# A decoder's quantised attention: projections in tiles of 128 rows, an eighth of the sequences carried by the others

## The reference

```python
def _ln(x, w, b):                       # mean and variance over the last axis
    return (x - mu) * jax.lax.rsqrt(var + EPS) * w + b
def _fp8_linear_pertensor(x, wq, w_scale, in_scale):
    xq = _div_clamp_fp8(x, in_scale)
    return jnp.einsum('bsi,oi->bso', xq * in_scale, wq) * w_scale
...
ln_out = _ln(hidden_states, ln_w, ln_b)
q = _ln(_fp8_linear_pertensor(ln_out, wq, ...).reshape(b, s, g, hpg, d), qln_w, qln_b)
k = _ln(_fp8_linear_pertensor(ln_out, wk, ...).reshape(b, s, g, d), kln_w, kln_b)
v = _fp8_linear_pertensor(ln_out, wv, ...).reshape(b, s, g, d)
core = _gqa(q, k, v).reshape(b, s, nh * d)          # softmax attention, no mask
qx = _ln(_fp8_linear_pertensor(ln_out, wqx, ...).reshape(b, s, g, hpg, d), qxln_w, qxln_b)
kvx = jnp.einsum('bsi,oi->bso', cond, w_kv_x)       # keys and values of the context
kx, vx = jnp.split(kvx, 2, axis=-1)
kx = _ln(kx.reshape(b, sc, g, d), kxln_w, kxln_b)
xout = _gqa(qx, kx, vx).reshape(b, s, nh * d)
catq = _div_clamp_fp8(jnp.concatenate([core, xout], axis=-1), proj_smooth)
return jnp.einsum('bsi,oi->bso', catq, wproj) * (proj_in_scale * proj_w_scale)
```

## Time and profile before

| | us |
|---|---|
| three runs | 3562.48, 3554.24, 3551.41 |
| median | 3554.24 |
| profiled execution | 3557.17 |
| its span | 3555.5 |
| self stage in it | 251 to 826 |
| cross stage in it | 826 to 2106 |
| first operation, before self | 17 to 251 |
| experts | 2106 to about 3000 |

### The profile page before, as it was taken

How to read it: one execution, slowest core, us unless ns; L and a number is a source line. 1 busy time by engine, 2 the same in 40 slices (tenths; PEclk the granted TensorE clock), 3 DMA queues, 4 the chain that set the end, 5 groups by cost and what they waited for, 6 DMA issues and landing times. The chain is left out here.

```text
span 3555.5 us, 54795 instructions
## 1 busy us (share of the span) xinstructions
PE 3301.0 (93%) x18088; PEld 2669.8 (75%) x18088; DVE 2445.3 (69%) x6438; ACT 1733.9 (49%) x4171; POOL 791.9 (22%) x897
## 2 busy tenths in 40 slices
PE   5858999997999999999999988999989889988999
PEld 4637877885777887778778866888878667767887
DVE  5998888886666666756666676899755555558332
ACT  5974454444344344443443432888547655541222
POOL 1003443442222222432222213000323410000000
PEclk9879999998999999999999999999999989999999
DMA  6130010002000000200000025999810133323000
GB/s 231 29 73 18 0 48 24 0 30 72 22 20 29 21 20 31 90 21 21 20 29 20 20 82 200 375 403 399 291 37 1 49 124 121 123 88 107 11 10 21
DMA packets 113586, 296.14 MB, mean 83 GB/s; under 512 B 37920, under 2 KB 42016, under 8 KB 107664
## 3 DMA queue, kind: packets, MB, share of 16 engines
q1 hardware_dynamic: 107264, 276.39, 22.0%
q0 software_dynamic: 6160, 17.67, 1.7%
HBM read 251.65 MB, written 41.68 MB: 83 GB/s over the span
## 5 line engine op out<-in xcount | busy, mean ns | idle before, releaser
L40 PE MATMUL bank<-w,cross_ctx_part 128*125 128x512 f32 x1536 | 516.9, 418 | 2.8 <-DVE cross_kn L1114 2.8
L40 PEld LDWEIGHTS bank<-w,cross_ctx_part 128*125 128x125 f32 x1536 | 282.2, 187 | 86.5 <-DVE cross_kn L1114 11.4
L1024 ACT ACTIVATE cross_prob<-bank,cross_neg_max 112x375 f32<-112x375 f32 x256 | 147.3, 575 | 358.9 <-DVE cross_neg_max L1120 358.9
L40 PE MATMUL bank<-w_low,cross_ctx_part 128*125 128x512 f32 x768 | 303.6, 395 | 0.0
L1120 DVE TENSOR_REDUCE cross_neg_max<-bank 112x1 f32<-112x375 f32 x256 | 134.1, 524 | 200.9 <-PE bank L892 198.3
L40 PE MATMUL bank<-moe_wt,moe_zT 128*128 128x448 f32 x1176 | 264.2, 373 | 2.1 <-DVE moe_zT L1785 1.5
L1775 DVE TENSOR_TENSOR moe_wt<-moe_raw,moe_wt 128x1792 fp32r<-128x1792 f32 (+1 forms) x111 | 231.9, 2109 | 14.9 <-ACT moe_wt L1673 13.8
L40 PE MATMUL bank<-w,self_xq 128*112 128x512 f32 x512 | 214.7, 419 | 20.9 <-DVE w_low L596 20.9
L40 PEld LDWEIGHTS bank<-moe_wt,moe_zT 128*128 128x128 f32 x1176 | 215.1, 190 | 17.6 <-issue 1.7
L40 PE MATMUL bank<-mlp_zT,mlp_signs 128*128 128x448 f32 x1024 | 220.6, 368 | 5.6 <-DVE mlp_zT L2465 5.6
L40 PEld LDWEIGHTS bank<-mlp_zT,mlp_signs 128*128 128x128 f32 x1024 | 193.4, 189 | 27.2 <-issue 5.9
(11 more groups left out here) (422 smaller groups left out, 8216.3 us busy)
## 6 DMA issues: line engine op xcount, KB each, us to landing
moe_raw<-in_moe_w SPq DMA_DIRECT2D x74, 896.0 KB, 7.4
moe_raw<-in_moe_w SPq DMA_DIRECT2D x37, 1024.0 KB, 8.5
stream<-in_L1f SPq DMA_DIRECT2D x32, 768.0 KB, 8.0
cross_ctx_raw<-in_ctxT SPq DMA_DIRECT2D x32, 750.0 KB, 4.2
wide_ctxT<-in_ctxT SPq DMA_DIRECT2D x16, 750.0 KB, 4.1
wide_ctx_rows<-in_ctx SPq DMA_DIRECT2D x16, 750.0 KB
expert_rows<-a_zeros SPq DMA_DIRECT2D x1, 8960.0 KB, 25.5
moe_zrow<-expert_rows SPq DMA_DIRECT2D x35, 256.0 KB, 7.7
```

The costliest lines, as they stand in the source:

```text
L40: mm = pe.matmul(out, a, b, start=first and n == 0, stop=last and n == len(pairs) - 1)
L1024: op = act.activation(prob[:, t % SLOTS, i, :], score_bank(t)[0:S, i * NK:(i + 1) * NK], ACT.Exp, bias=neg_max[:, h:h + 1], accum_out=tota ...
```

## The change

**Tiles of 128 rows.** The sequences go in groups of 8 (`GROUP`). The eighth of each (`spread(b)`: steps 7, 15, 23, 31 of each stage) has no query units of its own, and in self no key unit. Its 112 rows are dealt out to the seven others, 16 each (`EXTRA`), as the rows 112 to 127 of their tiles. `xq`, `qn`, `kn`, `qT` and in self `kT` become 128 wide, transposes of queries and of self keys have 128 columns. `keep_spread(b)` on GpSimd copies the 16 foreign columns from `kT` (self only) and `qT` to `spread_room`; the scores of the spread step read from there (`spread_qT`, `spread_kT`). Its values, and in cross its keys, are made as before.

**Inputs.** In self the cast is two operations, one for the own rows (`xq_main`) and one for the foreign 16 (`xq_ready`). In cross two transfers fill `xq_raw`, the second with 2 groups of 8 positions of the spread sequence.

**Order.** The step before a spread one has no units of the next sequence on PE in self; `project_out(b - 1)` moves up between the scores and the first turned probabilities, and `add_out(b - 1)` moves up on VectorE. The first `turn_probs` then waits for it. The spread step has no `turn` in self, and only that of the keys in cross.

**No loops.** All 32 steps of both stages are written out; counts become constants (`unit_no`, `norm_no`, `turned_no`, `tiles`). PE's program in these stages grows with it.

**Room.** In self `magic` moves into the second half of `probT` (so the second `take_probsT` waits for the rounding before), and in the last step its parts lie in `qn` and `spread_kT`. The new weights of a half are loaded when `unit_no` says that the last unit that reads them is done.

```diff
+    GROUP = 8
+    EXTRA = S // (GROUP - 1)
...
-        xq = sb("xq", [P, NV, DC, S], F32R)
+        xq = sb("xq", [P, NV, DC, P], F32R)
...
+        def over_loop(step):
+            for g in range(STEPS):
+                step(g, g < STEPS - 1)
+
+        def spread(b):
+            return b % GROUP == GROUP - 1
+
+        def has(b, n):
+            return not spread(b) or n >= (LU if own else 2)
+
+        def spread_rows(b):
+            return slice(EXTRA * (b % GROUP), EXTRA * (b % GROUP + 1))
...
+            def load_inputs(g):
+                raw = xq_raw[:].rearrange("p (t n) -> p t n", t=P // 8)
+                sp.dma_start(raw[:, 0:NT], io["xq_dram"][:, sequence(g)]).then_inc(k.xq_landed, 16)
+                sp.dma_start(raw[:, NT:], io["xq_dram"][:, spread_of(g), 2 * (g % GROUP):2 * (g % GROUP) + 2])\
                     .then_inc(k.xq_landed, 16)
...
+            def keep_spread(b):
+                pool.wait_ge(s["turned_ready"], turned_no(b, TG - 1 if own else 1))
+                if own:
+                    pool.tensor_copy(spread_kT[:, :, spread_rows(b)], kT[:, :, S:]).then_inc(s["spread_keys"], 1)
+                    pool.wait_ge(s["spread_keys"], tiles(b + 1))
+                pool.tensor_copy(spread_qT[:, :, spread_rows(b)], qT[:, :, S:]).then_inc(s["spread_ready"], 1)
...
                     if t == 0:
-                        wait(pe, s["x_done"], b - 1)
+                        wait(pe, s["x_done"], b if b < STEPS - 1 and spread(b + 1) else b - 1)
...
                 if own:
-                    turn(b)
+                    fills = one_more and not spread(b + 1)
+                    if not spread(b):
+                        turn(b)
                     unit(b, LU)
                     scores(b, 0)
                     scores(b, 1)
-                    if one_more:
+                    if fills:
                         unit(b + 1, 0)
                         unit(b + 1, 1)
+                    elif one_more:
+                        project_out(b - 1)
                     turn_probs(b, 0)
-                    if one_more:
+                    if fills:
                         unit(b + 1, 2)
                     turn_probs(b, 1)
...
                 if own:
-                    source = inputs[:, 0:2, bass.ds(sequence(b, base), 1)].rearrange("p v b c t -> p v (b c t)")
-                    act.activation(xq[:, 0:NQ].rearrange("p v c t -> p v (c t)"), source, ACT.Copy).then_inc(s["xq_ready"], 1)
+                    act.activation(xq[:, 0:NQ, :, 0:S], inputs[:, 0:2, sequence(b)], ACT.Copy).then_inc(s["xq_main"], 1)
+                    act.activation(xq[:, 0:NQ, :, S:], inputs[:, 0:2, spread_of(b), :, spread_rows(b)], ACT.Copy)\
+                        .then_inc(s["xq_ready"], 1)
...
+                    if early_out:
+                        add_out(b - 1)
```

346 lines of the change are left out of this document (188 added, 158 removed).

## The result

The changed kernel takes 3543.83 us (median of 11 runs, 3540.8 to 3548.6) where the kernel before takes 3558.42 (11 runs beside them, 3551.41 to 3562.48). The ratio is 0.9962, with a 95% interval of 0.9954 to 0.997: 14.6 us faster, about 0.4%.

A forecast was written before the change was run, and what follows sets the result against it. PE's instructions were taken to bound both edited stages until another chain takes over. Self +0.7 and cross +8.2 us, together 8.9, off the median 3554.2 gave 3545.3 us; range 3532 to 3560.

The forecast's parts named there:

- The chain of the self pair: Self step before a spread one: without the removed PE work, next scores at 13.55 instead of 16.29 us, 2.75 gained.
- The clock behind the self waits: Self pairs: PE's wait of 2.6 us halves the clock afterwards, costing 1.7 us at each of four places.
- rival A: Clock stays up in the self waits too, four times 1.7 us back: 3538; chance 0.20.
- The chain at sequence 15: Self, where halves change weights: VectorE's low parts leave at most 0.6 us gain, cold clock costs 1.7: -1.1.
- Sequence 31: Self: VectorE's own roundings end the stage; PE gains only the key unit's 1.9 us, less 1.7 for the clock: +0.2.
- Self tiles and loops: Self: 128-column transposes cost 4.2 us over 28 steps; writing out 24 looped steps gains 0.155 each, 3.7.
- Cross pairs: Cross step before a spread one and the spread step: 2.9 us gained at 7, 23, 31 and 2.3 at 15: +11.0.
- rival B: Clock also falls in the cross waits, 1.7 us for each of four: 3552, or 3547 to 3549; chance 0.16.
- Cross tiles: Cross: 8 wider transposes in each of 28 steps at 0.013 us each: -2.8.
- What was costed at nothing: Small cross input transfer, extra ScalarE cast in self, GpSimd's copies (0.35 and 0.5 us): all covered by idle time, 0 us.
- Rival C: GpSimd's copies are dear, delaying self tiles from 0.9 us each: 3560 at 1.3 each, 3593 at 1.90; chance 0.14.
- Rival D: Written-out code must be fetched, 0.2 us a step in 50 steps: 3555; chance 0.14 together with another rival.

The follow-up runs named there:

- the second execution: The changed kernel itself, unaltered, run and profiled again on the same chip beside the variants: 3556.78 us against 3572.86 for the kernel before, ratio 0.9958.

## Why the prediction was right

3545 was forecast from the median 3554.24 of three runs, a gain of 8.9. The measured gain is 14.6 and the time 3543.83, inside the range. That the time came within 1.5 us is luck in good part: the kernel before turned out at 3558.42, 4.2 above the base of the sum, and the gain was 5.7 larger, so two errors cancelled. The mechanism was right (which chain is left in a pair, what the tiles and the loops cost); the difference to the sum lies in few terms:

- **The chain of the self pair** (2.75): right. 2.68 in the warm pair, scores to scores 13.58 against 13.55, each step of the chain within 0.15. The wait was called 2.6, counted by starts; as a row's idle time, the measure in which the known 1.66 and 2.10 stand, it is 2.29. For the cross wait the sum had taken the last matmul's tail off, here it hadn't.
- **The clock behind the self waits** (1.7 at four places): here the sum failed. It took a wait of more than 2.10 as surely cold. Two of the four were cold (23 and 31), two warm (7 and 15), and a cold one costs 1.54; the written-out kernel even has a wait of 2.11 with the full clock behind it. The warm clock brought 1.6 at 7 and 1.6 at 15, which is half of rival A. At 15 the second execution had the fall, and was spared a later one.
- **The chain at sequence 15** (0.6 at most, -1.1 with the clock): 0.7 gained. VectorE's low part that releases's wait ends 22.58 behind the value copy of step 14 before and 21.65 now, 0.9 earlier.
- **Sequence 31** (+0.2): 0.87. With the wait filled the step is 14.55 instead of 16.95 before, so PE gained 2.4 where the sum had 1.9, and the clock cost 1.5 instead of 1.7.
- **Self tiles and loops** (-4.2 and +3.7): both right, apart: 24 ordinary steps at 0.17 are 4.1, and the run without loops shows 16.12 and 3.6 for the 24 steps. (16.29 - 16.12 is 0.17; the 0.155 of the sum is right for the mean of the looped steps, 16.27.)
- **Cross pairs** (2.9, and 2.3 at 15): 2.82, 2.84 and 2.13, and at 31 2.12 and the 0.7 behind the stage. The wait is 1.35 instead of 1.75: the first turning stands 0.63 behind the scores instead of the sum's 0.3, and the second 3.09 behind them instead of 3.2. The granted clock is 1.00 in windows behind all four waits (from 1103.8, 1410.3, 1734.6 and 2041.1 on), so rival B is refuted.
- **Cross tiles** (-0.10 a step): -0.11.
- **Cross step 0**: 1.45 gained that no term had, a fall of the clock that the kernel before had and this one hadn't. It isn't a merit of the change: five of the eight variants of the changed kernel have the fall again.
- **What was costed at nothing**: the copies at 0.63 and 0.29 (taken: 0.35 and 0.5) were covered, with 0.9 us to spare. The prediction had seen GpSimd's hold on VectorE, but not VectorE's on GpSimd, which makes 0.63 out of 0.24. Rival C's mechanism is real, as seven copies show, at a smaller price. Rival D is refuted by the written-out kernel, whose ordinary steps aren't longer.
- **A slip in the range**: rival A with the cheaper transposes gives 3545.3 - 6.8 - 1.7 = 3536.8, not 3535. It changes nothing.

The statement that most of the gain would be the cross pairs held (2.82 + 2.13 + 2.84, and 2.12 at 31: 9.9 us of 14.6). What the prediction didn't see is that the change carries an edit that works against it, the early projection. The sum had all the numbers for it: 13.55 was worked out for the early place, and 12.95 for the late one only afterwards.

## What to carry to other kernels

When work is taken off a packed engine, write out the chain that is left step by step, and do it for the old order as well as for the new one: the work that is moved into the hole may lengthen the very chain it was to shorten. Fill such a hole with work that is needed later and waits for nothing (here the next value unit and the next context unit, 14 and 7 us); that removes the wait and its clock together. And separate the parts of a change by a run of each alone: here one part (no loops) stood for nearly all of a stage's gain and hid that the other earned next to none. And count the falls of the clock in both traces before a difference of 1.6 us is given to the code.
